# Cross-attention keys that are never projected: queries taken through the key weights, key lengths by a triangular Gram product

## The reference

```python
features_n = rmsnorm(features, fn_w)              # features: the context
Q = rmsnorm(text @ Wq_w.T + Wq_b, qn_w)           # text: layer norm of x
K = rmsnorm(features_n @ Wk_w.T + Wk_b, kn_w)
attn = softmax(Q @ K.T / sqrt(512))
x = x + attn @ features_n
```

## Time and profile before

| what | us |
|---|---|
| median of three runs (3175.95 to 3185.04) | 3179.64 |
| the profiled execution, its own time | 3190.52 |
| its span in the trace | 3188.8 |
| the second attention, start to the end of the last weighted sum | 2479.1 to 2917.5 |
| of it the prologue, until the loop's first transpose | 57.4 |
| of it the four batches | 381.0 |

### The profile page before, as it was taken

How to read it: one execution, slowest core, us unless ns; L and a number is a source line. 1 busy time by engine, 2 the same in 40 slices (tenths; PEclk the granted TensorE clock), 3 DMA queues, 4 the chain that set the end, 5 groups by cost and what they waited for, 6 DMA issues and landing times. The chain is left out here.

```text
span 3188.8 us, 54146 instructions
## 1 busy us (share of the span) xinstructions
PE 3040.3 (95%) x18566; PEld 2702.9 (85%) x18566; DVE 2104.0 (66%) x3215; ACT 1733.4 (54%) x3277; POOL 908.0 (28%) x742
## 2 busy tenths in 40 slices
PE   8999998999999999999999999979989799998897
PEld 7888887899999999899998999968768788886786
DVE  4433343788888888788887888854454567766675
ACT  4433344676666666666666666642243344443472
POOL 0000121344444444444444444432200124440101
PEclk9999999999999999999999999999989799999998
DMA  7665696766777776677766777557540111111683
GB/s 253 216 214 200 207 289 200 152 159 161 165 160 158 163 157 164 150 165 158 160 160 155 160 158 163 127 148 238 190 160 32 57 29 41 41 41 30 236 289 129
DMA packets 375894, 497.03 MB, mean 156 GB/s; under 512 B 34316, under 2 KB 283452, under 8 KB 375640
## 3 DMA queue, kind: packets, MB, share of 16 engines
q1 hardware_dynamic: 373080, 485.40, 56.8%
q0 software_dynamic: 2560, 8.39, 0.8%
HBM read 225.57 MB, written 133.87 MB: 113 GB/s over the span
## 5 line engine op out<-in xcount | busy, mean ns | idle before, releaser
L725 POOL TENSOR_TENSOR a_t_lo<-a_turned,a_t_hi 128x512 fp32r<-128x512 f32 x512 | 649.7, 1291 | 937.9 <-ACT a_t_hi L854 937.9
L845 ACT ACTIVATE a_probs<-a_ps_s,a_neg_max 128x1024 f32<-128x1024 f32 (+1 forms) x512 | 529.2, 1034 | 474.7 <-DVE a_neg_max L897 468.8
L890 DVE TENSOR_REDUCE a_half_max<-a_ps_s 128x1 f32<-128x1024 f32 (+1 forms) x512 | 571.1, 1115 | 190.9 <-PE a_ps_s L742 186.7
L740 PE MATMUL a_ps_s<-a_k_buf,a_q_buf 128*128 128x512 f32 (+1 forms) x1024 | 420.1, 410 | 17.9 <-ACT a_probs L845 11.9
L741 PE MATMUL a_ps_s<-a_k_buf,a_q_buf 128*128 128x512 f32 (+1 forms) x1024 | 385.7, 377 | 0.0
L742 PE MATMUL a_ps_s<-a_k_buf,a_q_buf 128*128 128x512 f32 (+1 forms) x1024 | 384.8, 376 | 0.0
L926 DVE TENSOR_TENSOR a_x_lo<-a_ps_x,a_x_hi 128x512 fp32r<-128x512 f32 (+1 forms) x512 | 314.3, 614 | 106.6 <-ACT a_x_hi L863 106.6
L916 DVE STREAM_TRANSPOSE a_turned<-xn 128x512 f32<-128x512 f32 x512 | 357.4, 698 | 0.0
L472 DVE TENSOR_TENSOR p_out<-p_ps_j,p_out 128x512 fp32r<-128x512 f32 (+3 forms) x196 | 153.3, 782 | 302.4 <-ACT p_out L400 302.4
L400 ACT ACTIVATE p_out<-p_ps_j 128x512 fp32r<-128x512 f32 (+3 forms) x196 | 141.9, 724 | 311.4 <-PE p_ps_j L293 311.4
L740 PE MATMUL a_ps_o<-a_t_hi,a_v_buf 128*128 128x256 f32 x1024 | 298.8, 292 | 6.1 <-issue 3.6
(11 more groups left out here) (394 smaller groups left out, 7102.0 us busy)
## 6 DMA issues: line engine op xcount, KB each, us to landing
xn<-a_probs SPq DMA_DIRECT2D x1024, 128.0 KB, 3.4
a_q_all<-p_out SPq DMA_DIRECT2D x64, 512.0 KB
a_q_buf<-a_q_all SPq DMA_DIRECT2D x128, 256.0 KB, 3.2
a_k_buf<-a_k_all SPq DMA_DIRECT2D x64, 464.5 KB, 4.0
a_v_all<-p_out SPq DMA_DIRECT2D x56, 512.0 KB
a_k_all<-p_out SPq DMA_DIRECT2D x48, 384.0 KB
a_v_buf<-a_v_all SPq DMA_DIRECT2D x64, 256.0 KB
a_o_all<-a_o_part SPq DMA_DIRECT2D x128, 128.0 KB, 3.1
```

Source lines behind the costliest of these rows:

```text
L725: pool.tensor_tensor(t_lo[:, slot, :, :], turned[:, slot, :, :], t_hi[:, slot, :, :].bitcast(F32), ALU.subtract).then_inc(t_done, 1)
L740: pe.matmul(o, w_hi, m_hi, start=first, stop=False)
L845: act.activation(probs[j][u.a][:, lo:hi], s_flat[:, lo:hi], ACT.Exp, bias=neg_max[:, j:j + 1], scale=SCALE, accum_out=half_sum[:, bass.ds( ...
L890: dve.reduce_max(half_max[:, half:half + 1], s_flat[:, lo:hi], AX.X).then_inc(max_done, 1)
```

## The change

With the keys `K = F W + b` of scaled features `F` (here `W` is the turned key weight with `fn_w` multiplied in), a score is `(q W^T) F^T + q b`, and a key's squared length is `F G F^T + 2 F (W b) + b b`, with `G = W W^T`. So the keys are not formed. The queries, once normalised weights are multiplied in, pass through the key weights in the prologue (`through_keys`, 48 products of 256 columns a batch), and the turned features themselves take the keys' place in the scores. `G` is made once (`key_product`), as an upper triangle with its off-diagonal part doubled, `2 W b` and `b b` too (`key_bias`). For each tile twelve products of 512, 384, 256 and 128 columns (`key_products`) give features times `G`; DVE adds the bias row and multiplies by the features, with the sum of a row taken by the same instruction (`accum_out`). The lengths, one for each row, are turned by PE, rooted, inverted as rows of 128, and spread over the partitions by 13 float32 products with a selecting matrix (`spread_inverses`). The query's inverse length moves into the exponential's scale, and `q b` is summed by one-column products (`query_sums`: 48 records a batch where there were 16).

With it: the norm becomes part of the stage's own block, its tiles shared by DVE, ACT and POOL; the key weights, the vectors and the row `fn_w` are loaded in the experts' stage, where POOL multiplies the weights by `fn_w`, and the zeros are set there after the magnitudes in the same buffer; the ring has six tiles; scaling and the high part for the weighted sum move to ACT, the query's low part from DVE to POOL; query projections use two banks and the passage through the keys the other two; the probabilities are turned two groups ahead, and the next batch's first tile is turned and split at the end of the weighted sum. The diff, cut:

```diff
--- before.py
+++ after.py
+            sp.dma_start(key_w_rows[:, :, :], key_w.rearrange("(t p) d -> p t d", p=P)).then_inc(key_loaded, 16)
+            for i, column in enumerate(key_columns):
+                sp.dma_start(vectors[DC * i:DC * (i + 1), :], column.rearrange("(c p) -> c p", p=P)).then_inc(key_loaded, 16)
+            sp.dma_start(fn_row[:, :], key_columns[2].partition_broadcast(P)).then_inc(key_loaded, 16)
...
+            pool.wait_ge(magnitude_done, TILES)
+            pool.memset(zeros[:, :], 0.0).then_inc(zeros_set, 1)
+            pool.wait_ge(key_loaded, 16 * (2 + len(key_columns)))
+            for f in range(DC):
+                pool.tensor_tensor(key_w_rows[:, f, :], key_w_rows[:, f, :], fn_row[:, :], ALU.mult).then_inc(key_scaled, 1)
+            pool.wait_ge(key_scaled, DC)
...
-    RING = 4
...
+    RING = 6
...
-        norm_block(nc, held, x_res, xn, stats, 1e-5, "norm2", prefetch=load_weights)
...
+            for f in range(DC):
+                pool.wait_ge(w1_hi_done, f + 1)
+                pool.tensor_tensor(w1_lo[:, f, :], key_w[:, f, :], w1_hi[:, f, :].bitcast(F32), ALU.subtract).then_inc(w1_done, 1)
...
-                    pool.tensor_tensor(f_hi[0:n, t, :], raw[0:n, t % RING, :], ones[0:n, 0:1].to_broadcast([n, D]),
-                                       ALU.mult).then_inc(f_hi_done, 1)
...
+                    if t == 2:
+                        pool.wait_ge(q_hi_done, b + 1)
+                        pool.tensor_tensor(q_lo[:, :, :].rearrange("p c n -> p (c n)"), queries[:, bass.ds(b, 1), :].rearrange("p a n -> p (a n)"),
+                                           q_hi[:, :, :].rearrange("p c n -> p (c n)").bitcast(F32), ALU.subtract).then_inc(q_done, 1)
...
+            def key_product(f):
+                pe.wait_ge(w1_done, f + 1)
...
+                    mm = three(ps_s[:, c, c * P:D], w1_hi[:, f, c * P:(c + 1) * P], w1_lo[:, f, c * P:(c + 1) * P],
+                               w1_hi[:, f, c * P:D], w1_lo[:, f, c * P:D], f == 0, f == DC - 1)
+                    if f == DC - 1:
+                        mm.then_inc(g_ps, 1)
...
+            def through_keys(i):
+                pe.wait_ge(w2_done, DC)
+                pe.wait_ge(qt_done, DC * (i + 1))
+                for c in range(DC):
+                    if DC * i + c >= 2:
+                        pe.wait_ge(q_kept, DC * i + c - 1)
+                    else:
+                        pe.wait_ge(g_done, sum(len(g_parts(c)) for c in range(DC)))
+                    for f in range(DC):
+                        mm = three(ps_s[:, 2 + c % 2, 0:TOK], w2_hi[:, f, c * P:(c + 1) * P], w2_lo[:, f, c * P:(c + 1) * P],
+                                   qt_hi[i % 2][:, f, :], qt_lo[i % 2][:, f, :], f == 0, f == DC - 1)
+                    mm.then_inc(qk_ps, 1)
+
...
                 for j in range(QT):
+                    at = QT * i + j
                     for f in range(DC):
-                        mm = pe.matmul(ps_p[:, 0, QT * i + j:QT * i + j + 1], squared[i % 2][:, f, j * P:(j + 1) * P], ones[:, 0:1],
-                                       start=f == 0, stop=f == DC - 1)
+                        pe.matmul(ps_p[:, 0, at:at + 1], squared[i % 2][:, f, j * P:(j + 1) * P], ones[:, 0:1],
+                                  start=f == 0, stop=f == DC - 1)
+                    for f in range(DC):
+                        pe.matmul(ps_p[:, 1, at:at + 1], qt_hi[i % 2][:, f, j * P:(j + 1) * P].bitcast(F32), z_col[:, f:f + 1],
+                                  start=f == 0, stop=False)
...
+            key_product(0)
+            key_product(1)
+            key_bias()
+            transpose_weights(0)
+            transpose_weights(1)
+            key_product(2)
+            transpose_weights(2)
+            key_product(3)
+            transpose_weights(3)
...
+                    through_keys(i - 1)
+                    query_sums(i - 1)
+            pe.wait_ge(xt_done, TILES)
+            transpose_features(0, 0)
+            through_keys(B - 1)
+            query_sums(B - 1)
             pe.wait_ge(set_up, 3)
...
+                def key_products(t):
+                    n = rows_of(t)
+                    pe.wait_ge(ft_done, KT * b + t + 1)
+                    if t == 0:
+                        pe.wait_ge(s_scaled, PRIMED + 2 * QT * b)
+                    if t >= 4:
+                        pe.wait_ge(y_added, KT * b + t - 3)
+                    for c in range(DC):
+                        m_hi, m_lo = (g[:, g_at[c]:g_at[c] + D - c * P] for g in (g_hi, g_lo))
+                        mm = three(ps_s[0:n, t % 4, c * P:D], k_hi[:, c, t * P:t * P + n], k_lo[:, c, t * P:t * P + n],
+                                   m_hi, m_lo, c == 0, c == DC - 1)
+                    mm.then_inc(norm_ps, 1)
...
+                    pe.transpose(ps_p[0:hi - lo, 1, 0:P], key_norm[:, lo:hi], ident[:, :]).then_inc(kt_ps, 1)
+
+                def spread_inverses(h):
+                    lo, hi = KEYS[h]
+                    pe.wait_ge(k_inv, 2 * b + h + 1)
+                    for t in range(lo, hi):
+                        mm = pe.matmul(ps_p[:, t // GROUP % 2, t % GROUP * P:(t % GROUP + 1) * P], pick[0:hi - lo, t - lo, :],
+                                       key_row[0:hi - lo, h, :], start=True, stop=True)
...
+                        transpose_features(t + 1, KT * b)
+                    key_products(t)
+                    if t == FIRST + 1:
+                        turn_norms(0)
+                spread_inverses(0)
...
+                scores(0, 1)
+                scores(0, 0).then_inc(s_ps, 1)
+                scores(0, 2)
+                turn_norms(1)
+                scores(0, 3).then_inc(s_ps, 1)
+                spread_inverses(1)
+                scores(1, 0)
+                scores(1, 1).then_inc(s_ps, 1)
+                transpose_probs(0, 0)
+                transpose_probs(0, 1)
+                scores(1, 2)
+                scores(1, 3).then_inc(s_ps, 1)
                 pe.wait_ge(f_done, KT * (b + 1))
...
+                    if n + 2 < len(steps):
+                        transpose_probs(*steps[n + 2])
+                    elif n == len(steps) - 1:
+                        pe.wait_ge(pt_done, PRIMED + GROUPS * QT * b + n)
+                        transpose_features(0, KT * (b + 1))
                     weigh(j, g)
...
+                for t in range(KT):
+                    n = rows_of(t)
+                    if t + 2 < KT:
+                        scale_tile(b, t + 2)
+                    if t + 1 < KT:
+                        features_hi(b, t + 1)
+                    if t == 0:
+                        act.wait_ge(o_ps, PRIMED + QT * b)
+                    act.wait_ge(f_scaled, KT * b + t + 1)
+                    act.activation(f_hi[0:n, t, :], raw[0:n, t % RING, :], ACT.Copy).then_inc(f_hi_done, 1)
+                    if t == 1:
+                        act.activation(q_hi[:, :, :].rearrange("p c n -> p (c n)"), queries[:, bass.ds(b, 1), :].rearrange("p a n -> p (a n)"),
+                                       ACT.Copy).then_inc(q_hi_done, 1)
+                    if t == FIRST + 3:
...
+                def key_sum_of(t):
+                    n, held_at = rows_of(t), biased[t % 2]
+                    dve.wait_ge(norm_ps, KT * b + t + 1)
+                    dve.tensor_tensor(held_at[0:n, :], ps_s[0:n, t % 4, :], u_row[0:n, :], ALU.add).then_inc(y_added, 1)
+                    dve.wait_ge(y_added, KT * b + t + 1)
+                    dve.scalar_tensor_tensor(held_at[0:n, :], held_at[0:n, :], 1.0, raw[0:n, t % RING, :], ALU.mult, ALU.mult,
+                                             accum_out=key_sum[0:n, t:t + 1]).then_inc(sum_kept, 1)
...
+                    dve.reciprocal(key_row[0:hi - lo, h, :], key_row[0:hi - lo, h, :]).then_inc(k_inv, 1)
...
+                    dve.scalar_tensor_tensor(probs[j][:, lo:hi], s_flat[:, lo:hi], q_now[:, CQ, j:j + 1], key_inv[:, lo:hi],
+                                             ALU.add, ALU.mult).then_inc(s_scaled, 1)
...
-                        dve.scalar_tensor_tensor(k_lo[:, f, c0:c0 + w], ps_s[:, f, 0:w], columns[:, BK, f:f + 1],
-                                                 k_hi[:, f, c0:c0 + w].bitcast(F32), ALU.add, ALU.subtract).then_inc(k_done, 1)
...
-                    dve.tensor_tensor(sq[:, 0:2, :], sq[:, 0:2, :], sq[:, 2:4, :], ALU.add).then_inc(k_added, 1)
...
-                    dve.reciprocal(key_inv[:, lo:hi], key_inv[:, lo:hi]).then_inc(k_inv, 1)
...
+                for t in range(KT):
+                    if t + 1 < KT:
+                        features_lo(b, t + 1)
+                    key_sum_of(t)
+                    if t == FIRST - 1:
+                        key_norms(0)
+                    if t == KT - 2:
+                        invert(0)
+                key_norms(1)
+                dve.wait_ge(now_done, b + 1)
+                scale_scores(0, 0)
+                invert(1)
+                scale_scores(0, 1)
+                largest(0)
```

(58 more changed lines are left out.)

609 lines of the change are left out of this document (303 added, 306 removed).

## The result

The changed kernel takes 3188.08 us in the median of 16 runs (3184.14 to 3190.69), the kernel before 3179.24 (16 runs, 3175.95 to 3185.06). The ratio is 1.0027 with a 95% interval of 1.0019 to 1.0034: 8.8 us slower, small but clear of noise, where 10 us faster was forecast.

A forecast was written before the change was run, and what follows sets the result against it. PE, busy 95% of the span, was taken as the bound nearly everywhere, with DVE close behind. Prologue +54 and four batches -64 gave -10 us on the 3179.64 median: 3170, range 3150 to 3206.

The forecast's parts named there:

- the clock paragraph: Prologue: four runs of 48 one-column records would each be followed by a fall of PE's clock, 16 us together.
- rival 1: Prologue: the clock holds through the sums, 16 us come back, giving 3154 us; chance 0.18.
- 4 for each of four: 16: Prologue: 4 us lost to a clock fall for each of four runs of sums, between 1.5 and 5.3 us.
- +54: Prologue: 112 us forecast against 57.4 before, from 96 at full clock plus 16 for falls.
- two to four times 0.23: Prologue, bias row: price of each of four float32 products of 512 columns; 4.4 us with four one-column sums.
- 79.3: Each batch: forecast us against 95.25 before, 16 less a batch and 64 less in four.
- 13 float32 picks ...: 2.9: Each batch, after the tiles: picks spreading the inverses, two records each at 0.11 us, 2.9 us in all.
- 24.4: Each batch: us for probabilities and weighted sum, 25.4 before, less one of 2 us of wait through earlier transposes.
- lag: Each batch's tiles: 0.3 us for DVE's lag when stretched beside POOL and PE's tile waits, making 31.2.
- rivals 2 and 3: Rival 2: DVE's accumulating product at half rate, 3198 us, chance 0.20; rival 3: 128-column products cost as 512-column, 3190, 0.14.
- Rival 4: Tiles: half-rate accumulating DVE product and 128-column products at the 512-column price together, 3214 us; chance 0.08.
- What costs nothing: Experts' stage: added loads, POOL multiplications and zeros are covered; the slots' clearing keeps some 80 us until the changed stage.

The follow-up runs named there:

- e2: Changed kernel with each query batch's 24 one-column sums in four portions of six behind groups of wide products: 3173.54 us, ratio 0.9980 to the kernel before.
- e3: Changed kernel with 20 instead of 48 records of one-column sums a batch, seven of eight key-bias parts left out: 3168.30 us.
- e1: Changed kernel with the first eight picks issued behind the first chunk of scores instead of ahead of it: 3180.49 us.
- e5: Changed kernel with sums in portions, first picks behind a scores chunk, last five between wide chunks, DVE's second reciprocal ahead of its first scaling: 3175.62 us.
- e4: Changed kernel with POOL's feature subtraction cut to 64 of 512 columns except in the last tile: 3182.79 us.
- e9: Changed kernel with sums in portions, both pick groups moved, POOL's subtraction behind DVE's accumulating product, first probabilities turned later: 3152.38 us, ratio 0.9914 to the kernel before.
- e6: Changed kernel with sums in portions, both pick groups moved, and POOL's subtraction waiting for DVE's accumulating product: 3171.33 us.
- e8: Changed kernel with sums in portions, only the first picks moved, and POOL's subtraction waiting for DVE's accumulating product: 3161.19 us.

## Why the prediction was wrong

**The prologue: right mechanism, term too large.** A fall came with each of the four runs of sums, as the clock paragraph had it, and rival 1 (no fall) is out. The falls set in within the runs: the records stand 0.11 us apart at first and 0.21 at the end of each run. The term "4 for each of four: 16" was mis-sized: order alone was worth 11.1 us in the prologue (e2), 2.8 each. That is nearly all of the 5 by which +54 exceeded the measured +49. (The fourth fall ran on into the first batch, with a clock of 0.50 until 2590.0, which costs some 2 us there.) The prices of records hold within 1 us: 28 fewer in each of four batches, with the falls, gave 23.0 of 24 (e3). No row of the kernel before shows the "two to four times 0.23" of the bias row, whose 4.4 us came out at 4.3 (2486.91 to 2491.20).

**The batches: the step that failed.** 79.3 was forecast, 84.7 measured in the second batch. Cut as the forecast cut it: tiles 31.2 against 32.15; first eight picks 1.8 (of the 2.9 for thirteen) against 3.4; scores with five picks and the two first turns 20.0 + 1.1 + 1.0 = 22.1 against 25.3; weighted sum 23.4 against 22.9; head 0.8 against 1.0. So:

- The step "13 float32 picks ...: 2.9" priced PE's records and nothing ahead of or behind them. Ahead stood the chain of the last tiles' products on DVE and its first reciprocal, 1.41 us of idle PE, where the forecast looked for such a wait only at the second turn (0.7 us, measured 0.16). A wait for the spread inverses beyond 0.7 us was among its own signs of being wrong. Behind the picks stood the clock.
- The clock was charged in the prologue alone. The forecast knew from the earlier trace rows that PE falls to the lower level behind a run of thin records, and it put another run of them, with an idle stretch before it, ahead of the scores' wide products without asking. Both falls together are the 3.2 us by which the scores of this batch miss (half of the time at the lower level). e1 takes wait and first fall away in three batches of four (-2.9 in the second); e5 takes both falls away in two of four, shown by the clock at 1.00, and pays with a longer wait. The other batches of the first profile have one fall each in the scores, short or long.
- Falls were not new to the batches. The weighted sum of the earlier trace rows has one (0.93 over 25.4 us, some 1.7 us), and the forecast carried it over in its 24.4; afterwards that stretch runs at 1.00. Over all four batches the mean clock is 0.95 before and 0.96 after, by estimate some 19 and 13 us lost, where the forecast's terms hold 7.
- The tiles' 0.3 us for "lag" was 1.6 by e4: POOL and DVE do meet. The cover that was called thin was thin; still, PE is busy for 30.1 of the tiles' 32.15 us.

64 - 44.8 = 19.2 us missing in the batches, 5 won in the prologue: the stage went from a forecast of -10 to +5 in the first profiles. That 3188 lies within the stated range is luck: the range reached that far up for rivals 2 and 3, and both are out. Rival 4's 3214 does not follow from its parts either: with PE's tile at 2.78 us, DVE at 2.9 to 3.05 is only 0.12 to 0.27 over it, which gives 3196 to 3204. **What costs nothing** held: the slots' clearing was issued 3.6 us later (2374.34) and landed after 29.0, far ahead of the stage. The change holds a gain that its order gave back: in e9's order the same work is 27 us faster than the kernel before.

**Open.** Some 2 us of the 8.8 lie outside the stage in the means of two profiles, and their cause is not shown. 1.3 of them are there when the experts' stage ends: at 2477.4 and 2477.0 before, at 2477.9 and 2479.0 after. In the eleven profiles of the changed kernel and its variants that point lies between 2476.6 and 2483.7, and most of this spread is there already early in the experts' stage (its first low part of the tokens starts at 2321.0 to 2328.9), ahead of everything in which these kernels differ. The profiles of e3, e5, e6 and e8 also have a last stage of 261 to 263 us in place of 257 to 260, which takes back some of the gain there; its cause was not tried. Nor was it tried how much the kernel before, which has falls and waits of its own, would gain from such orders; so e9 does not say how the two arithmetics compare at their best.

## What to carry to other kernels

Cost a thin run of TensorE (one-column sums, products on a few rows) with what follows it: price its records, the wait ahead of it, and the wide products behind it at the lower clock, which does not come every time; then put it in portions between wide work, where the same instructions cost 11 us less here. A wait that is taken off PE shows the next one on the same chain (e5 to e9), so look at what the moved instructions feed before moving them. And cut two profiles of each kernel by stage before comparing spans: one execution here was 11 us off in a stage that nobody had touched.

## What the runs showed of the hardware

A DVE product of two float32 SBUF tiles with a summed output took 693 ns in the median for 128x512, and 81 ns more for the read-out: 774 against 752 without the sum, not twice as long. TensorE counted as busy for every microsecond of the one-column sums, and its granted clock still fell within each run of 48 records; of four runs of 20, two were followed by a fall, and 12 at a time between wide products left it at 1.00. Float32r products of 66 and 256 columns start 0.11 to 0.12 us apart; of three of 128 columns in a row, the second starts 0.06 us behind the first, and the others follow at 0.11 to 0.12.
